# Second feed-forward: the residual of thirteen pairs moves from TensorE's accumulation to an add on POOL

## What is computed

```
def fp4_linear(x, w): return fp4_quant_dequant(x) @ fp4_quant_dequant(w).T
gate = fp4_linear(x, w_gate); y = fp4_linear(x, w_up)      # 128 -> 352
h = silu(gate) * y
ffn = fp4_linear(h, w_down)                                # 352 -> 128
x = x + ffn
```

## Time and profile before

| what | value |
|---|---|
| median of 3 executions | 644.71 us |
| the profiled execution, its own time | 645.09 us |
| its span, first to last instruction | 643.0 us |
| PE busy | 580.1 us (90% of the span) |
| DVE busy | 481.7 us (75%) |
| ACT busy | 352.5 us (55%) |
| POOL busy | 306.4 us (48%) |
| mean granted TensorE clock | 0.981 |

### The profile page before, as it was taken

One profiled execution on the slowest core, in us unless ns is written; L12 is line 12 of the kernel. 1 busy time (PEld: TensorE's weight loads), 2 busy tenths in 40 slices (PEclk: granted clock), 3 DMA queues, 4 the chain that ended last, 5 costly groups with the idle time before them and its releaser, 6 DMA issues.

```text
span 643.0 us, 14032 instructions
## 1 busy us (share of the span) xinstructions
PE 580.1 (90%) x5407; PEld 427.5 (66%) x5407; DVE 481.7 (75%) x1008; ACT 352.5 (55%) x662; POOL 306.4 (48%) x353
## 2 busy tenths in 40 slices
PE   4989998799999999879999888999999988699996
PEld 4878886466666689846767665555566555477775
DVE  6768886566666645889998667777777775899972
ACT  5742331344444452368998745444544446699973
POOL 6442111222232224466787566444555335577763
PEclk9999999799999999989999979999999999799999
DMA  9500000000000000000000000000000000001011
GB/s 246 132 2 1 3 3 1 1 1 1 2 1 2 2 17 19 2 0 2 2 0 2 2 0 2 2 1 2 2 3 1 1 3 2 1 17 34 17 34 33
DMA packets 15908, 9.56 MB, mean 15 GB/s; under 512 B 1446, under 2 KB 15718, under 8 KB 15844
## 3 DMA queue, kind: packets, MB, share of 16 engines
q1 hardware_dynamic: 15844, 8.68, 5.2%
HBM read 6.59 MB, written 2.10 MB: 14 GB/s over the span
## 4 chain that ended last, share of the span: by engine, by line
PE 44%; DVE 21%; POOL 11%; ACT 11%; issue 11%; DMA 1%; POOLq 0%; SPq 0%; DVEq 0%; ACTq 0%
PE ps L1276 6%; PE ps L1435 4%; PE ps L1292 4%; PE ps L1452 4%; PE ps L1476 4%; PE ps L1457 3%; PE ps L1546 3%; DVE r L892 3%; DVE m L936 3%; PE ps L1283 3%; ACT S L542 2%; POOL arena L422 2%; POOL G L328 2%; ACT qbd L571 2%; PE ps L1468 2%
## 5 line engine op out<-in xcount | busy, mean ns | idle before, releaser
L387 POOL TENSOR_TENSOR A<-S,r 126x512 f32<-126x512 f32 x36 | 37.7, 1048 | 147.4 <-DVE r L895 134.0
L422 POOL TENSOR_SCALAR_AFFINE_SELECT arena<-arena 128x1024 f32<-128x1024 f32 x32 | 35.9, 1121 | 70.2 <-ACT arena L726 70.1
L328 POOL TENSOR_TENSOR G<-S,hoff 128x704 f32<-128x704 f32 x32 | 48.6, 1520 | 34.1 <-DVE S L1032 32.1
L1452 PE MATMUL ps<-wguT,xnt 128*128 128x352 f32 x128 | 52.6, 494 | 13.3 <-ACT xnt L635 11.9
L726 ACT ACTIVATE arena<-ps 128x1024 f32<-128x1024 f32 x32 | 32.7, 1022 | 46.6 <-PE ps L1546 46.6
L1476 PEld LDWEIGHTS ps<-wdT,xnt 128*128 128x128 f32 (+1 forms) x384 | 51.3, 196 | 8.6 <-ACT xnt L642 2.6
L1476 PE MATMUL ps<-wdT,xnt 128*128 128x128 f32 (+1 forms) x384 | 55.0, 280 | 1.9 <-ACT xnt L642 1.9
L1117 DVE TENSOR_TENSOR arena<-ps,XN 128x1024 f32<-128x1024 f32 x32 | 39.2, 1224 | 17.2 <-PE ps L1546 17.2
L892 DVE TENSOR_REDUCE r<-S 126x16 f32<-126x512 f32 x36 | 24.7, 685 | 34.1 <-ACT S L542 34.1
L1457 PE MATMUL ps<-wguT,xnt 128*128 128x352 f32 x128 | 45.5, 480 | 0.2 <-DVE S L1032 0.2
L546 ACT ACTIVATE arena<-ps 128x456 f32<-128x456 f32 x36 | 19.9, 552 | 41.4 <-PE ps L1292 41.4
(11 more groups left out here) (201 smaller groups left out, 1512.4 us busy)
## 6 DMA issues: line engine op xcount, KB each, us to landing
X<-in_x SPq DMA_DIRECT2D x8, 256.0 KB, 5.3
out<-X SPq DMA_DIRECT2D x8, 256.0 KB, 2.3
arena<-in_wqkvT SPq DMA_DIRECT2D x4, 256.0 KB, 5.4
band<-in_band SPq DMA_DIRECT2D x1, 897.8 KB
arena<-in_wqkvT SPq DMA_DIRECT2D x1, 512.0 KB, 8.7
early<-in_wfc SPq DMA_DIRECT2D x1, 512.0 KB, 10.4
kI<-in_scaled_eye SPq DMA_DIRECT2D x1, 192.0 KB
XN<-in_wattn SPq DMA_DIRECT2D x1, 192.0 KB, 2.4
```

The source lines that it names most:

```text
L328: tt(out=hgrid, in0=hmoved[k], in1=hoff[k][:, :], op=ALU.subtract).then_inc(s["fh_grid"], 1)
L387: tt(out=A1v[:, w % NW, :].rearrange("p (h m) -> p h m", m=M), in0=S1v[:, w % NW, :].rearrange("p (h m) -> p h m", m=M), in1=r1[:, 3, w % ...
L422: nc.gpsimd.affine_select(out=masked[n % 2][:, 8:16, :], in_=raw.rearrange("p (h t) -> p h t", t=P), pattern=[[0, 8], [1, P]], compare_op= ...
L1452: mm(ps[:, GATE_BANK, 0:F], xT[t // QD % 2][:, t % QD, :], wguT[:, 0:F], start=True, stop=True).then_inc(s["f_gate"], 1)
```

## The change

For the first 13 pairs (`BY_POOL` = `PN` - 3) of pass 1 only, `down_mms` leaves out the identity product with `X` and closes the accumulation with the last down product. `down_copy` copies the bare down products to one of two new SBUF buffers, `delta[r % 2]`, and counts a new semaphore, `f_copied`; before it writes a buffer it waits until POOL has added the pair two before. POOL adds `delta` to `X` and counts `f_x_done`. POOL does this for pair `r` - 3 as the first thing in its step `r`. `h_transposes` waits on `f_copied` in place of `f_x_done`, which is still counted up by ScalarE's copy. Pairs 13 to 15 stay with TensorE; their `down_copy` waits until the earlier pairs are counted, so that `f_x_done` stays in order. Nothing else is altered.

```diff
+BY_POOL = PN - 3
...
+        delta = [part(2 * P).rearrange("p (k c) -> p k c", k=2) for _ in range(2)]
...
+                def residual(r):
+                    n = ffn_pairs(p, r)
+                    g.wait_ge(s["f_copied"], r + 1)
+                    tt(out=X[:, 2 * r:2 * r + 2, :], in0=X[:, 2 * r:2 * r + 2, :], in1=delta[r % 2], op=ALU.add).then_inc(s["f_x_done"], 1)
+
                 def step(r):
                     q = (r + FILL) // 2
+                    if p == 1 and 0 <= r - 3 < BY_POOL:
+                        residual(r - 3)
                     if r % 2 and q < QN:
                         quantise_x(q)
...
                 def down_copy(r):
                     n = ffn_pairs(p, r)
                     a.wait_ge(s["f_down"], n + 1)
-                    act(X[:, 2 * r:2 * r + 2, :], ps[:, T_BANK + 1, 0:2 * P].rearrange("p (k c) -> p k c", k=2), ACT.Copy).then_inc(s["f_x_done"], 1)
+                    moved = ps[:, T_BANK + 1, 0:2 * P].rearrange("p (k c) -> p k c", k=2)
+                    if p == 1 and r < BY_POOL:
+                        need(a, "f_x_done", n - 1 if r > 1 else 0)
+                        act(delta[r % 2], moved, ACT.Copy).then_inc(s["f_copied"], 1)
+                    else:
+                        if p == 1:
+                            a.wait_ge(s["f_x_done"], n)
+                        act(X[:, 2 * r:2 * r + 2, :], moved, ACT.Copy).then_inc(s["f_x_done"], 1)
...
-                        if k == 1:
+                        if k == 1 and p == 1 and 0 < r <= BY_POOL:
+                            pe.wait_ge(s["f_copied"], r)
+                        elif k == 1:
                             need(pe, "f_x_done", n)
...
+                        added = p == 1 and r < BY_POOL
                         for c in range(3):
                             last = mm(ps[:, T_BANK + 1, k * P:(k + 1) * P], hT[r % 2][0:FK[c], k, c, :], wdT[0:FK[c], c, :],
-                                      start=(c == 0), stop=False)
-                        last = mm(ps[:, T_BANK + 1, k * P:(k + 1) * P], eye[:, :], X[:, 2 * r + k, :], start=False, stop=True)
+                                      start=(c == 0), stop=added and c == 2)
+                        if not added:
+                            last = mm(ps[:, T_BANK + 1, k * P:(k + 1) * P], eye[:, :], X[:, 2 * r + k, :], start=False, stop=True)
```

## The result

The changed kernel took 650.66 us (median of 8) against 644.63 us for the kernel before (median of 8, run beside it): a ratio of 1.0097, 95% interval 1.0075 to 1.0119. It is slower by about 6 us. The profiled execution took 650.39 us with a span of 648.3 us, 5.3 us more than before.

What follows compares the result with a forecast made beforehand. A loop of ACT's copy, PE's transposes and gate, and ACT's silu was taken to bound up to step 10, TensorE from step 11. 5.08 + 0.96 - 0.45 = 5.59 us slower gave 650.3 us, range 647.6 to 652.9.

Steps and rivals of the forecast that it cites:

- The add: POOL's add of 256 columns, ahead of quantise_x in odd steps: priced at 0.79 us.
- Transposes to gate: PE in an odd step, from the band transposes to the gate product, unhindered: 0.81 us.
- Gate to D: From the odd step's gate product to D, the end of the even step's down-product copy: 5.10 us as before.
- The turn: Two steps of the new loop ACT, POOL, PE, ACT: 12.06 us instead of 10.79.
- The sum: Whole kernel: 5.08 us for four turns, 0.96 in step 11, less 0.45 in step 13: 5.59 us slower.
- The identity products were worth nothing before step 11: PE's saving of 0.45 us a pair counts for nothing up to step 10, hidden by the loop.
- The even steps' adds are hidden: Adds in even steps and steps 12 to 14 delay nobody; in the latter 3.84 us against 4.25 available.
- PE's share: PE's busy share in the slowed double steps falls from 99% to some 87%.
- TensorE as the bound throughout: Rival: TensorE bounds everywhere, so all 13 pairs give 0.45 us: 638.9 us, faster; chance 0.04.
- Only the wait counts: Rival: add of nearly no time, 1.64 us slower, 646.3 us; partial form 3.8 us, 648.5 us; chance 0.12.
- POOL's wait is covered: Rival: the add fits POOL's 1.05 us of idle time, only 0.90 us saved at the end: 643.8 us; chance 0.04.
- The dear add: Rival: POOL's add takes 1.27 us, giving 652.7 or 652.9 us; chance 0.15.

Runs made afterwards that it cites:

- no_residual: Kernel before without the identity products of pairs 0 to 12 in the second feed-forward, nothing in their place: stage 77.01 us, 1.09 us shorter than before.
- odd_pairs: The change for the odd ones of the first thirteen pairs only, the even ones keeping the identity product: double step 10.80 us, stage 0.65 us shorter.
- add_last: The changed kernel with POOL's add behind quantise_h instead of ahead of quantise_x (pair 12's stays first): 0.9977 of the kernel before, stage 77.01 us.
- wait_only: Kernel before plus POOL's wait for the copy of pair r - 3, without any add: double step 11.37 us, stage 3.06 us longer.

## Why the prediction was right

It gave 650.3 us and slower with 0.91; measured were 650.66. That these two lie 0.4 us apart shows little, given 4.7 us between the fastest and the slowest of the eight executions; the difference of the medians is 6.0 us, interval 4.8 to 7.7, with the forecast 5.59 inside. The steps of the sum show more. Step by step, the predicted value first:

- **ACT to POOL:** 0.07; 576.74 to 576.82, 0.08.
- **The add:** 0.79, then `quantise_x`. Its rows read 0.73, and L320 starts 0.69 after it. The price was 0.1 too high.
- **`quantise_x` to the `band` operand:** 5.24; 577.51 to 582.75, 5.24. **POOL to PE:** 0.05, and 0.05.
- **Transposes to gate:** 0.81; 582.80 to 583.51, 0.71. My 0.81 came from a step in which the second half of the transposes had still waited for ACT's copy. It wasn't the unhindered pace.
- **Gate to D:** 5.10 "as before"; 583.51 to 588.79, 5.28. Here a wait appeared that I had not seen: with the transposes late, ACT's `hT_copy` (L651) is late too, PE's `x` transposes wait 0.19 us for it, and ACT's next copy 0.35 us for them.
- **The turn:** 12.06, and 12.05. Two errors cancelled, 0.19 us too long before the gate and 0.18 too short behind it; that it agrees to 0.01 is luck, that it agrees to a few tenths is not.
- **The sum:** four turns 5.08, and 5.00 measured (48.19 - 43.19 from D of step 2 to D of step 10); step 11 with its saving 0.96, and 11.29 - 10.37 = 0.92; from there to the end -0.45, and 24.12 - 24.54 = -0.42. Together 5.59 forecast, 5.50 measured. In step 11 errors cancelled again: the gate was 1.22 us late (619.66, 6.77 after D), not 1.41, and 0.30 us was had back behind it, not 0.45.
- **The identity products were worth nothing before step 11:** shown by `no_residual`. 52 of 128 of their instructions went, as said.
- **The even steps' adds are hidden:** shown by `odd_pairs`. For steps 12 to 14 the margin was worked out from a wrong length: 9.40 us in the earlier trace rows isn't two steps, from copy to copy they are 10.06. Less the saving, a step is 4.58 (4.59 measured), not 4.25. L333 ended 0.55 us before PE came to it in step 13 and 0.05 before in step 14. The last three stretches of `no_residual`, without adds, are the same as those of `add_last` within 0.02 us, and the last two as those of the change.
- **PE's share:** I said 87% of the double step; it is 9.93 of 12.05, 82%. 87% doesn't follow from the prediction's own numbers: 10.72 less 0.90, of 12.06, is 81%.

The rivals: TensorE as the bound throughout was refuted by `no_residual`. "Only the wait counts" gave 1.64 us of loss for a free add with TensorE's saving. `wait_only` has no saving, and shows 3.06; its four ordinary turns cost 0.57 us each where I had 0.48 (578.01 to 584.10 is 6.09 us before the gate where I had 6.17, and from there to D 5.29 where I had 5.10, as above). That POOL's wait is covered is refuted by the 2.49 us that POOL stands idle before L339. The dear add falls with its row, 0.73 us.

## What to carry to other kernels

Before an operation is moved to an engine with spare time, compare two time stamps: when its input is ready, and when the operation behind it in that engine's queue used to start. Here the input came 0.84 us later, and a wait at the head of an in-order queue held up work on which everybody depends, and closed a new loop over three engines; the same add behind the quantisation of `h` is free. And an engine that is 99% busy need not bound: what a saving there is worth is seen by what the operation that sets the pace waits for last, stage by stage, and best by a run with nothing but the saving in it.

## What was not expected of the hardware

The add of 256 columns took 0.73 us and that of 512 (L417) 1.269: by these two rows an estimate of 2.1 ns a column and some 0.19 us fixed. The slope from the 1824-column row, 1.88, with a larger fixed part, had given 0.79. The Trainium skill, GPSIMD Engine Reference, section Elementwise — side-by-side cycle accounting, states about 2.6 cycles an element at 1.2 GHz, 2.2 ns as an estimate from that page: as a slope it agrees with these two rows, as the whole time (0.55 us) it is too low. DVE's rows didn't grow beside the adds: L1048, which runs beside the add of an odd step (576.54 to 577.42), took 883 ns on average in the changed kernel, as L1032 before.
